# Deformable sampling: the sum over four corners is taken by TensorE while it transposes

## What is computed

```python
val = corner(y0i, x0i, (1 - fy) * (1 - fx)) + corner(y0i, x0i + 1, (1 - fy) * fx) \
    + corner(y0i + 1, x0i, fy * (1 - fx)) + corner(y0i + 1, x0i + 1, fy * fx)
...
g = deform_sample(x, py, px) * mask[:, :, None]
wr = dc_w.reshape(dc_w.shape[0], DG, Cc // DG, K)
out = jnp.einsum('odck,bdckhw->bohw', wr, g)
```

## Time and profile before

| | |
|---|---|
| median of 3 runs | 4872.33 us (4863.74 to 4876.03) |
| span of the profiled execution | 4881.7 us |
| busy TensorE, VectorE, ScalarE, GpSimd | 3089.0, 3063.1, 2265.4, 1416.5 us |
| first and last indirect DMA of the sampler | 3073.3 and 4857.4 us |
| GpSimd busy on them | 1183.7 us |
| multiply L1746 and reduce L1751, 64 each | 164.0 and 260.4 us |
| transposes L1805, 320 | 81.1 us |

### The profile page before, as it was taken

The page is one execution under the profiler, slowest core; times in us unless marked ns, Lnnn a source line. Parts: engine busy times, 40 slices in busy tenths (PEclk is TensorE's granted clock), DMA queues, the critical chain, the costliest instruction groups (busy, mean ns, idle before and its releaser), DMA issues. The chain is left out here.

```text
span 4881.7 us, 56324 instructions
## 1 busy us (share of the span) xinstructions
PE 3089.0 (63%) x21212; PEld 1439.3 (29%) x21212; DVE 3063.1 (63%) x3884; ACT 2265.4 (46%) x1769; POOL 1416.5 (29%) x1213
## 2 busy tenths in 40 slices
PE   3566648899999997999999997233225223611012
PEld 2456624233333333233333334111112111310001
DVE  5989953999999993999999993222413332332113
ACT  1344421799999992899999990000000000000000
POOL 3800000200000002000000000666666676667756
PEclk7677768899999998999999998666556555655555
DMA  2200000000000000000000000212111211211111
GB/s 41 80 0 0 0 1 3 1 2 1 1 1 2 2 1 0 1 1 1 1 1 2 2 1 18 53 40 59 38 47 39 56 50 43 53 44 53 49 34 43
DMA packets 125524, 105.90 MB, mean 22 GB/s; under 512 B 100288, under 2 KB 102464, under 8 KB 125292
## 3 DMA queue, kind: packets, MB, share of 16 engines
q0 software_dynamic: 36864, 75.57, 5.7%
q1 hardware_dynamic: 86796, 26.43, 2.4%
q10 hardware_dynamic: 1632, 0.56, 0.1%
HBM read 82.50 MB, written 19.96 MB: 21 GB/s over the span
## 5 line engine op out<-in xcount | busy, mean ns | idle before, releaser
L1322 PE MATMUL PS<-adder_layer_Z,c_adder_out 128*32 128x512 f32 x16896 | 1850.8, 595 | 107.1 <-DVE adder_layer_Z L1387 56.7
L1357 ACT ACTIVATE adder_layer_Z<-adder_layer_CP,AN 128x2048 f32 x984 | 1873.5, 2019 | 88.3 <-PE PS L1322 87.5
L1387 DVE TENSOR_SCALAR adder_layer_Z<-adder_layer_CP,AW 128x2048 f32 x1128 | 1421.8, 1327 | 119.7 <-ACT adder_layer_CP L1346 70.9
L1695 POOL DMA_INDIRECT sampler_G<-neighbours,sampler_IDX x1152 | 1183.7, 1027 | 714.6 <-issue 347.4
L1322 PEld LDWEIGHTS PS<-adder_layer_Z,c_adder_out 128*32 128x32 f32 x16896 | 655.7, 110 | 1301.9 <-issue 1183.1
L1826 ACT ACTIVATE sampler_VT<-PS 128x512 f32<-128x512 f32 x64 | 38.2, 597 | 1141.7 <-PE PS L1805 659.9
L1805 PE MATMUL PS<-c_ident,sampler_VAL 128*128 128x128 f32 (+1 forms) x320 | 81.1, 416 | 733.3 <-DVEq L1753 702.5
L1394 DVE SCALAR_TENSOR_TENSOR adder_layer_Z<-adder_layer_CP,AW,adder_layer_Z 128x1024 f32<-128x1024 f32 x384 | 476.4, 1282 | 34.7 <-issue 34.7
L1813 PE MATMUL PS<-sampler_VT,DC 128*64 128x128 f32 (+1 forms) x640 | 162.0, 424 | 409.1 <-issue 289.7
L1751 DVE TENSOR_REDUCE sampler_VAL<-sampler_G 128x576 f32<-128x2304 f32 x64 | 260.4, 4069 | 131.6 <-remote 107.4
L1746 DVE TENSOR_TENSOR sampler_G<-sampler_G,sampler_W 128x2304 f32<-128x2304 f32 x64 | 164.0, 2562 | 269.1 <-DMA sampler_G<-neighbours,sampler_IDX 260.5
(11 more groups left out here) (346 smaller groups left out, 2623.5 us busy)
## 6 DMA issues: line engine op xcount, KB each, us to landing
sampler_G<-neighbours,sampler_IDX POOLq DMA_INDIRECT x1152
neighbours<-top_k_zero SPq DMA_DIRECT2D x16, 578.0 KB, 6.7
neighbours<-sampler_HT SPq DMA_DIRECT2D x256, 32.0 KB, 1.6
X<-in_x SPq DMA_DIRECT2D x8, 256.0 KB, 6.1
out<-X SPq DMA_DIRECT2D x8, 256.0 KB
P<-in_L_conv_conv_w SPq DMA_DIRECT2D x4, 144.0 KB
P<-in_L_conv_add_w SPq DMA_DIRECT2D x4, 144.0 KB
RAW<-in_L_conv_w SPq DMA_DIRECT2D x4, 144.0 KB
```

The source lines that it names most:

```text
L1322: mm = t.matmul(PS[32 * j:32 * j + 32, k, :], K["adder_out"][:, 32 * i:32 * i + 32], Z[:, r % SLOTS, j, c:c + BANK], start=False, stop=Fal ...
L1357: op = a.activation(z(r, j), seen(ch, ty, tx), ACT.Relu, bias=ANf[:, weight(ty, tx, j, i)])
L1387: op = v.tensor_scalar(z(r, j), seen(ch, ty, taps[0]), AWf[:, weight(ty, taps[0], j, i)], 0.0, ALU.subtract, ALU.max)
L1695: g.indirect_dma_start(G[th % RING][:, k, :], None, tables[b], bass.IndirectOffsetOnAxis(ap=IDX[:, b % 2, step, k:k + 1], axis=0))\
```

## The change

It removes the reduce. VectorE writes the products to a new tile `PROD`, corner by corner, and signals `val` at once; GpSimd waits on `val` in place of `used`. The wait on `t_ps` now stands ahead of the multiply, since it writes what TensorE reads. TensorE replaces each of the five transposes of a step by four ordinary float32 matmuls against the identity that accumulate in PSUM. To make room, `OFF` shares its memory with `T`.

```diff
-            VAL = sb("VAL", [128, 2, GK, CG])
+            PROD = sb("PROD", [128, 2, 4, GK, CG])
...
-            H2, OFF = sb("H2", [128, PX]), sb("OFF", [128, PX])
+            H2, OFF = sb("H2", [128, PX]), T
...
-                            g.wait_ge(used, th - RING + 1)
+                            g.wait_ge(val, th - RING + 1)
...
-                        g3 = gt[:, :, :].rearrange("p k (q c) -> p (k q) c", q=4)
-                        v.tensor_tensor(g3, g3, w4.rearrange("p k q -> p (k q)").unsqueeze(2)
-                                        .broadcast_to([128, GK * 4, CG]), ALU.mult)
-                        v.drain()
                         if th >= 2:
                             v.wait_ge(t_ps, th - 1)
-                        v.tensor_reduce(VAL[:, th % 2, :, :], gt[:, :, :].rearrange("p k (q c) -> p k c q", q=4),
-                                        AX.X, ALU.add)
+                        v.tensor_tensor(PROD[:, th % 2, :, :, :].rearrange("p q k c -> p k q c"),
+                                        gt[:, :, :].rearrange("p k (q c) -> p k q c", q=4),
+                                        w4.unsqueeze(3).broadcast_to([128, GK, 4, CG]), ALU.mult)
                         v.drain().then_inc(val, 1)
-                        v.sem_inc(used, 1)
...
-                        flat = VAL[:, th % 2, :, :].rearrange("p k c -> p (k c)")
+                        flat = PROD[:, th % 2, :, :, :].rearrange("p q k c -> p q (k c)")
...
-                            mm = t.transpose(PS[0:n, th % 2 if c < 4 else 2, o:o + 128],
-                                             flat[:, 128 * c:128 * c + n], K["ident"][:, :])
+                            for q in range(4):
+                                mm = t.matmul(PS[0:n, th % 2 if c < 4 else 2, o:o + 128],
+                                              flat[:, q, 128 * c:128 * c + n], K["ident"][:, :],
+                                              start=(q == 0), stop=(q == 3))
```

More of the change, by code:

```diff
@@ L1487, in sampler @@
             arrived = [sem(f"arrived{i}") for i in range(RING)]
-            used, val, t_ps, t_sb, d_ps, d_sb, leaky, e_ps, e_sb, final, written = (
-                sem(n) for n in ("used", "val", "t_ps", "t_sb", "d_ps", "d_sb", "leaky", "e_ps", "e_sb", "final",
+            val, t_ps, t_sb, d_ps, d_sb, leaky, e_ps, e_sb, final, written = (
+                sem(n) for n in ("val", "t_ps", "t_sb", "d_ps", "d_sb", "leaky", "e_ps", "e_sb", "final",
                                  "written"))
```

## The result

The changed kernel takes 5045.15 us (median of 4 runs, 5033.52 to 5062.60), the kernel before beside it 4868.03 (4856.99 to 4876.03): a ratio of 1.0392, 95% interval 1.0342 to 1.0443, so some 177 us slower. The forecast was 5245 with a range of 4970 to 5520. The direction holds, and so does the count of instructions behind it; the forecast loss of 373 us was about twice the measured one, and the stock of the prediction turned out not to be a fixed number.

The account below looks back on a forecast made before the run. GpSimd's gathers set the steps, and TensorE's results, one per 1.40 us during gathers, force pauses. 37 pauses at 17 us, 629, less 254 before, add 375 to 4872: 5247, stated as 5245, range 4970 to 5520.

Parts of the forecast that it names:

- the stock: In sampling, some 126 TensorE instructions that pass before results slow to one per 1.40 us; GpSimd's pauses restore it.
- the pace: In sampling, while GpSimd issues gathers, TensorE's results become visible at one instruction per 1.40 us.
- Reduce off the steady step: VectorE's reduce, 4.07 us a step, ends 13 us before the next gather lands; removing it there is worth nothing.
- Reduce off the end of each pause: Where GpSimd waits for a buffer behind multiply and reduce, removing the reduce is worth 11 x 4.1 = 45 us.
- Multiply with its output apart: VectorE's multiply into a separate tile takes 2.56 us; if strided and stretching GpSimd's DMAs, up to 96 us more.
- Count of instructions: TensorE in sampling goes from 30 to 100 instructions a step, 3020 to 7500 in all.
- The number of pauses: GpSimd's buffer waits: 6403 instructions beyond the slow rate, at 175 each, make 37 instead of 11.
- The price of a pause: Each GpSimd buffer wait costs 17 us instead of 23.1, from release 3.5, products 9, copy 1.4, multiply 2.6.
- A: Rival: the per-instruction limit spares these products or never bites; each of 11 pauses ends 4.1 us sooner, 4827; chance 0.11.
- B: Rival: the saving and TensorE's longer step cancel at the 11 pauses; time within 0.3% of 4872; chance 0.05.
- C: Rival: each of the 64 sampling steps has its own pause of 23.1 us, +1224, 6096 us; chance 0.08.
- D: Rival: products stay at one load-matmul pair each, 60 instructions a step, 22 pauses at 17, 4992 us; chance 0.09.

Follow-up runs that it names:

- `v_only`: Changed kernel's VectorE, but five transposes of one corner a step on TensorE, the other three left out: 4650.93 us beside the kernel before at 4653.48, ratio 0.9995.
- `early_free_2`: Kernel before, but the multiply writes to its own tile and frees the gather buffer at once; reduce and transposes stay: 4827.27 us beside 4868.32, ratio 0.9910.
- `after`: The changed kernel in its first comparison with the kernel before: 5045.15 us beside 4868.03, ratio 1.0392.
- `after_b`: The changed kernel, nothing further altered, run again beside the kernel before on another chip: 4655.99 us beside 4653.02, ratio 1.0005.

## Why the prediction was right, and where it was off

**What bounds the kernel.** Right, with a limit that the rows of one execution could not show: the pauses belong to chips on which the pace occurs. On two others the unchanged kernel takes 4651 to 4653 us; every kernel with gathers that was traced there, the changed one and those with one part alone, has no pauses. (The reduce ends 17 us before the next gather lands, not 13; nothing hangs on it.)

**Reduce off the steady step: nothing.** Right; without the pace, `v_only` removes it and gains nothing (0.9995).

**Reduce off the end of each pause: 45 us.** Right in size; `early_free_2` gains 41, 3.5 us a pause and one pause fewer.

**Multiply with its output apart: 2.56 us.** Right (2563 ns mean). The 96 us of a strided multiply did not arise; the range, though the prediction says so, did not hold them either (4872 + 697 = 5569). The mean DMA fell from 1027 to 1015 ns.

**Count of instructions.** Right: 7500, and two pairs for each product (2560 records). The fourfold price of a product against a transpose, which the Trainium skill gives (TensorE: Matmul & The Clock Gate, "Terms"), would have made 21 us of a step's products; the trace has 4.9 to 6.2 in the stretch shown, and at one clock (0.50) five chunks took 1.33 us as transposes and 2.58 us as matmuls, twice and not four times. Execution was sized too high: 9 us for 40 pairs was worked out from rows at a granted clock of 0.50, the lower of the two levels, 1.2 GHz (by these rows it should even have been 10, some 40 us more in the forecast). After a pause TensorE now runs without gaps, the clock is granted at 0.92, most of the stretch at the upper level, 2.4 GHz, and the pairs take 4.9 to 6.2 us.

**The number of pauses is the step that failed:** "37 pauses instead of 11". It rested on 175 instructions for each pause. Measured are 20 pauses. GpSimd was active for 1941 - 427 = 1514 us, 1081 instructions at 1.40; the other 6419 make 321 a pause. Behind the 175 stands the stock, which the prediction took for a fixed number, 126. The kernel before gives that number again in its next two pairs (copies at 3991.76 and 4445.33, each 89.9 us after the resume). The changed kernel doesn't (timeline from 3478):

```profile
3478.64 3.26 POOL L1695 DMA_INDIRECT sampler_G<-neighbours,sampler_IDX  x1 [22.66 <-DVEq L1750]
...
3514.20 5.82 PE L1802 MATMUL PS<-c_ident,sampler_PROD 128*128 128x128 f32 x40
...
3524.64 0.60 ACT L1824 ACTIVATE sampler_VT<-PS 128x512 f32<-128x512 f32 x1 [13.03 <-remote]
```

GpSimd doesn't pause between these lines, and TensorE executes 240 pairs, 480 instructions, up to the end of the products in the second of them. All are visible 46.0 us after the resume, of which the pace accounts for 33; some 447 got past it. In the stretch from 3844.66, shown above, 216 were visible after 16.8 us (the copy at 3861.45), but the next 80 not before 78.6 us, while SyncE's stores went at the same pace. So the stock is not a fixed number of TensorE's instructions, and a sum that takes it for one can't count the pauses. What sets it I did not find.

**The price of a pause,** 17 us, measured 427.1/20 = 21.4. Too low, for two chains that the sum didn't have: it counted only products, copy and multiply. At a bank's end the pause holds L1811, the scale, the 1x1 convolution and `U` before the next multiply (20.3 us at 3935.73). Three of the four longest pauses, 33.3 to 34.3 us, hold a stage's convolution, for which the prediction allowed half a microsecond. Before the resume at 3844.66, with its 33.33 us, stands

```profile
3819.19 0.60 ACT L1824 ACTIVATE sampler_VT<-PS 128x512 f32<-128x512 f32 x1 [39.57 <-remote]
...
3822.53 16.16 PE L1510 MATMUL PS<-P,WB 128*128 128x512 f32 x36
```

and VectorE's part of that stage. Too many pauses at too low a price: the two errors pull against each other, 20 x 21.4 = 428 where 37 x 17 = 629 was forecast.

**Signs.** Two that the prediction named for itself did not come: GpSimd's waits were 427.1 us in 20 pieces, not 500 to 700 in over 25, and most of VectorE's wait ahead of the multiply was still ended by the gather (332.9 of 497.0 us), not by TensorE.

**Rivals.** A (the saving alone, 4827) and B (it cancels) describe what happens without the pace, though not for their reasons: there is no saving to be had either. The argument held against A, that 20, 30 and 2 instructions give 1.40 us each, stands on chips with the pace. A's example, code fetching, does grow with the change, and is answered below. C (every step pays) is out: 20 pauses, not 64. D is out by the record count.

**What stays open** is what in a chip makes the pace. The traces tie it to stretches in which GpSimd issues gathers, to a fixed 1.40 us for an instruction of any size, to results held back while execution is shown as done, to some chips and not others, and to SyncE's issues as well as TensorE's. Code fetching is not late. Every page lists the packets that fetch code; on one queue one of 16 KB comes for every 256 or so of TensorE's instructions, and its line (packets, MB, share of 16 engines) is the same with the pace (`after`) and without (`after_b`):

```profile
q8 instruction: 193, 3.16, 0.3%
```

In the sampling phase both traces have 29 of them, which last 1.07 and 1.02 us on average and start after the same number of TensorE's instructions to within 20. The Trainium skill (NOTIFIC — the notification-queue block, "7.1 Overflow: three behaviours, one of which stalls the engine") names a way in which the writing of an engine's records could stall it. No run here tests that: every execution on record, the timed ones too, lists its span and granted clock, so none was taken without records. Whether plain DMAs bring the pace on a chip that has it is open too, since both runs of that kernel met chips without it.

## What to carry to other kernels

Count a change's instructions on each engine, not only its busy time: here 70 more small instructions a step on TensorE, which was far from full, cost 4% where each had a price of its own, and the 260 us taken off VectorE had been hidden under the gather but for some 41. When the result of an instruction is used long after its record ends, look for what holds it back, on the other engines too, and ask whether it has a price per instruction. And time the unchanged kernel on more than one chip before a loss or a gain in such a phase is called a property of the program.

## What I had not expected of the hardware

The same program took 4868 to 4870 us in three comparisons and 4651 to 4653 in three others, 4.7% apart, while within one comparison the runs of the kernel before stay within 0.8% of their median; the pairs of loads 2.80 us apart are there in the sampling phase of every trace of the former and of none of the latter. While it lasts, the pace is the same 1.40 us for matmuls of 128 and of 512 columns, for their weight loads, and for SyncE's issues of stores.
